# Coupled harmonics and the one-hot's counting row read from PSUM by VectorE; the weighted sweeps' one-hot compare made per tile

## The reference, cut to what matters

```
edge_index = stack([src, dst])
x = layernorm(x + L0(x, edge_index, edge_attr_4, edge_attr_32, ...))     # weighted: per-edge MLP gives 4 x 8 x 8 weights
x = layernorm(x + L1(x, edge_index, edge_weight1, edge_attr_3, edge_attr_5, W))   # coupled
x = layernorm(x + L2(x, edge_index, W1, b1, W2, b2))                     # two convolutions
x = layernorm(x + L3(x, edge_index, edge_attr_4, edge_attr_8, ...))      # weighted, MLP of three layers

# coupled layer: harmonics sh (1 + 3 + 5 values per edge) times the source's features, mixed by W
for idx, (le, ln, lo) in enumerate(COMBOS):
    base = einsum('ijk,ei,emj->emk', CG[le, ln, lo], sh[le], feats[ln])
    msg[lo] = msg[lo] + einsum('io,eik->eok', W[idx], base)
agg0 = segment_sum(msg[0], dst);  agg1 = segment_sum(msg[1], dst)
```

## Time and profile before

| | |
|---|---|
| median of 3 runs | 26496.01 us (26398.16 to 26498.13) |
| profiled execution, first to last instruction (span) | 21541.2 us |
| profiled execution, time outside its span | not recorded |
| PE / weight loads | 13199.4 us busy (61%) / 9916.4 (46%) |
| DVE | 9294.4 us (43%) |
| ACT | 2665.2 us (12%) |
| POOL | 15690.7 us (73%) |
| mean granted TensorE clock | 0.678 of 2.4 GHz |

### The profile page before, as it was taken

The page is one execution under the profiler, slowest core; times in us unless marked ns, Lnnn a source line. Parts: engine busy times, 40 slices in busy tenths (PEclk is TensorE's granted clock), DMA queues, the critical chain, the costliest instruction groups (busy, mean ns, idle before and its releaser), DMA issues. The chain is left out here.

```text
span 21541.2 us, 268058 instructions
## 1 busy us (share of the span) xinstructions
PE 13199.4 (61%) x71680; PEld 9916.4 (46%) x71680; DVE 9294.4 (43%) x22443; ACT 2665.2 (12%) x6512; POOL 15690.7 (73%) x15707
## 2 busy tenths in 40 slices
PE   8999999976666666512222223212221399999999
PEld 5666666666666666511111112111111266666666
DVE  7777777833333333211111111111111388888885
ACT  2333333310000000100000000000000022222222
POOL 6777777747777777677777774777777677777774
PEclk8988988955555555555555555555555599999997
DMA  1111111111111111100000010000000111111111
GB/s 32 26 26 26 26 26 26 27 13 16 16 16 16 16 16 16 15 14 14 14 14 14 14 13 12 14 14 14 14 14 14 15 17 18 18 17 18 17 17 13
DMA packets 1290570, 372.67 MB, mean 17 GB/s; under 512 B 1002127, under 2 KB 1269819, under 8 KB 1290172
## 3 DMA queue, kind: packets, MB, share of 16 engines
q0 software_dynamic: 502400, 258.23, 7.7%
q1 hardware_dynamic: 788150, 114.20, 3.3%
HBM read 363.02 MB, written 8.00 MB: 17 GB/s over the span
## 5 line engine op out<-in xcount | busy, mean ns | idle before, releaser
L323 POOL DMA_INDIRECT conv_rows<-conv_rows,conv_idx x6280 | 5927.4, 944 | 2245.2 <-issue 1912.6
L753 PE MATMUL conv_win<-conv_onehot,conv_rows 128*32 128x64 f32 x12560 | 1572.6, 312 | 6305.3 <-DMA conv_rows<-conv_rows,conv_idx 6254.9
L753 PEld LDWEIGHTS conv_win<-conv_onehot,conv_rows 128*32 128x32 f32 x12560 | 1298.6, 169 | 6579.0 <-issue 4974.1
L323 POOL DMA_INDIRECT coupled_rows<-x_after_weighted,coupled_idx x3140 | 3302.0, 1052 | 1206.1 <-issue 955.0
L323 POOL DMA_INDIRECT weighted_rows<-in_x,weighted_idx x3140 | 3251.5, 1036 | 1105.3 <-issue 937.4
L323 POOL DMA_INDIRECT weighted_rows<-x_after_convolved,weighted_idx x3140 | 3209.0, 1022 | 1064.2 <-issue 953.7
L458 PE MATMUL weighted_weights_ps<-weighted_w_out,weighted_hidden 128*128 128x256 f32 x12580 | 3781.5, 426 | 21.1 <-DVEq L550 21.1
L669 PE MATMUL coupled_win<-coupled_onehot,coupled_prod 128*125 128x64 f32 x12560 | 2762.0, 418 | 1531.0 <-DVE coupled_prod L705 1531.0
L669 PEld LDWEIGHTS coupled_win<-coupled_onehot,coupled_prod 128*125 128x125 f32 x12560 | 2677.4, 330 | 1615.6 <-issue 834.5
L458 PEld LDWEIGHTS weighted_weights_ps<-weighted_w_out,weighted_hidden 128*128 128x128 f32 x12580 | 2256.0, 199 | 1818.0 <-issue 1617.9
L767 DVE TENSOR_TENSOR acc<-acc,conv_win 32x64 f32 x1256 | 262.3, 209 | 6237.3 <-PE conv_win L753 6237.3
(11 more groups left out here) (133 smaller groups left out, 8636.9 us busy)
## 6 DMA issues: line engine op xcount, KB each, us to landing
conv_rows<-conv_rows,conv_idx POOLq DMA_INDIRECT x6280, 2.3
weighted_feat<-in_ef SPq DMA_DIRECT2D x632, 80.0 KB
weighted_rows<-in_x,weighted_idx POOLq DMA_INDIRECT x3140
coupled_rows<-x_after_weighted,coupled_idx POOLq DMA_INDIRECT x3140, 2.3
weighted_rows<-x_after_convolved,weighted_idx POOLq DMA_INDIRECT x3140, 2.3
weighted_idx<-in_src_blocks SPq DMA_DIRECT2D x1264, 2.5 KB
weighted_sh<-in_sh SPq DMA_DIRECT2D x1264, 10.0 KB
conv_idx<-in_src_blocks SPq DMA_DIRECT2D x1264, 2.5 KB, 1.6
```

The costliest lines, as they stand in the source:

```text
L323: pool.indirect_dma_start(rows[s][:, t, :], None, table, bass.IndirectOffsetOnAxis(ap=idx[s][:, t:t + 1].bitcast(U32), axis=0))\
L753: mm = pe.matmul(win_ps[s % 2][0:FEAT, 0:WINDOW], rows[s][:, t, :], onehot[s][:, t, :], start=(t == 0), stop=(t == TILES - 1))
```

## The change

Three edits:

1. In the coupled sweep the harmonics are staged to PSUM. A new ACT program waits for a slot's load, and then copies the slot's `sh` (128 x 45) to one of two PSUM tensors `sh_ps`; the copy for block n + 2 is made when the message of block n is ready. DVE's two products read `sh_ps` in place of `sh` and wait for `sh_ready` in place of `loaded`.
2. In the coupled sweep and the convolutions the counting row is a PSUM tensor. The compare keeps its form.
3. In the weighted sweeps the counting row stays in SBUF. The compare of a block is five `tensor_scalar` operations of 64 columns, one per tile, in which the local target is a per-partition scalar operand, in place of one `tensor_tensor` of 320.

```diff
--- before.py
+++ after.py
@@ -332,7 +332,7 @@
 
         self.dve, self.k, self.iota, self.base_f, self.base, self.stepped = dve, k, iota, base_f, base, stepped
         dve.memset(k["acc"][0:parts[0], 0:parts[1], :], 0.0).then_inc(stepped, 1)
-        dve.tensor_copy(iota[:, :], k["iota0"][:, :]).then_inc(stepped, 1)
+        dve.tensor_copy(iota, k["iota0"][:, :]).then_inc(stepped, 1)
         dve.memset(base_f[:, :], float(NODES)).then_inc(stepped, 1)
         dve.wait_ge(stepped, 3)
         dve.tensor_copy(base_f[:, 1:BLOCKS + 1], k["lo"][:, :]).then_inc(stepped, 1)
@@ -343,7 +343,7 @@
     def next_window(self, p):
 
         dve = self.dve
-        dve.tensor_scalar(self.iota[:, :], self.iota[:, :], float(WINDOW), None, ALU.add).then_inc(self.stepped, 1)
+        dve.tensor_scalar(self.iota, self.iota, float(WINDOW), None, ALU.add).then_inc(self.stepped, 1)
         dve.tensor_scalar(self.base_f[:, :], self.base_f[:, :], float(WINDOW), float(NODES), ALU.add, ALU.min)\
            .then_inc(self.stepped, 1)
         dve.wait_ge(self.stepped, p * 3 + 7)
@@ -353,6 +353,14 @@
     def bases(self, block, count=SLOTS):
 
         return nc_values(self.k["nc"], self.base[0:1, bass.ds(block + 1, count)])
+
+    def one_hot_tiles(self, dst, block):
+
+        for t in range(TILES):
+            last = self.dve.tensor_scalar(
+                dst[:, t, :], self.iota,
+                self.k["local"][:, bass.ds(block, 1), t:t + 1].rearrange("p b t -> p (b t)"), None, ALU.is_equal)
+        return last
 
     def one_hot(self, dst, block):
 
@@ -545,7 +553,7 @@
                 dve.wait_ge(params, PARAMS)
                 dots = w_out[0:HID + 1, 0:2 * MUL * MUL].rearrange("h (o q i) -> h o q i", q=2, i=MUL)[:, :, 0, :]
                 dve.tensor_scalar(dots, dots, float(1 / np.sqrt(3.0)), None, ALU.mult).then_inc(ones, 1)
-                win = Windows(dve, k, iota, base_f, base, stepped, (P, 2))
+                win = Windows(dve, k, iota[:, :], base_f, base, stepped, (P, 2))
                 dve.sem_inc(summed, 1)
                 dve.sem_inc(w_used, 2)
 
@@ -569,7 +577,7 @@
                             x, h, scaled = rows[s], sh[s], scaled_pair[s % 2]
                             harm = h[:, :, 1:4][:, :, None, :].broadcast_to([P, TILES, MUL, 3])
                             vecs = x[:, :, MUL:].rearrange("p t (i m) -> p t i m", m=3)
-                            win.one_hot(onehot[s], i * SLOTS + s).then_inc(vec, 1)
+                            win.one_hot_tiles(onehot[s], i * SLOTS + s).then_inc(vec, 1)
                             dve.wait_ge(gathered[s], g * (16 * TILES) + 16 * TILES)
                             dve.wait_ge(loaded[s], g * 48 + 48)
 
@@ -633,8 +641,12 @@
         idx, sh = ring("idx", [P, TILES], I32), ring("sh", [P, TILES, HARM])
         rows, onehot = ring("rows", [P, TILES, FEAT]), ring("onehot", [P, TILES, WINDOW])
         prod = ring("prod", [P, TILES, 2 * OCH])
-        iota, base_f, base = sb("iota", [P, WINDOW]), sb("base_f", [1, BLOCKS + SLOTS]), sb("base", [1, BLOCKS + SLOTS], I32)
+        base_f, base = sb("base_f", [1, BLOCKS + SLOTS]), sb("base", [1, BLOCKS + SLOTS], I32)
         win_ps = [ctx.enter_context(nc.psum_tensor(f"coupled_win{b}", [P, 512], F32)) for b in range(2)]
+        iota = ctx.enter_context(nc.psum_tensor("coupled_iota", [P, 512], F32))[:, 0:WINDOW]
+        sh_ps = [ctx.enter_context(nc.psum_tensor(f"coupled_sh_ps{b}", [P, 512], F32))[:, 0:TILES * HARM]
+                 .rearrange("p (t c) -> p t c", c=HARM) for b in range(2)]
+        sh_ready = sem("sh_ready")
         loaded, gathered = [sem(f"loaded{s}") for s in range(SLOTS)], [sem(f"gathered{s}") for s in range(SLOTS)]
         msg_ready, spread, summed, stepped, ones = sem("msg_ready"), sem("spread"), sem("summed"), sem("stepped"), sem("ones")
         started, ended = sem("started"), sem("ended")
@@ -671,6 +683,21 @@
                                                start=(t == 0), stop=(t == TILES - 1))
                         mm.then_inc(spread, 1)
 
+            @block.scalar
+            def _(act):
+                def stage(s, turn):
+
+                    act.wait_ge(loaded[s], turn * 32 + 32)
+                    nc.scalar.activation(sh_ps[s % 2], sh[s][:, :, :], ACT.Copy).then_inc(sh_ready, 1)
+
+                turns = Turns(act, k)
+                stage(0, 0)
+                stage(1, 0)
+                with turns.flat() as g:
+                    for s in range(SLOTS):
+                        act.wait_ge(msg_ready, g * SLOTS + (s + 1))
+                        stage((s + 2) % SLOTS, g + (s + 2) // SLOTS)
+
             @block.vector
             def _(dve):
                 for s in range(SLOTS):
@@ -694,10 +721,10 @@
                         bases = win.bases(i * SLOTS)
                         for s in range(SLOTS):
                             n = g * SLOTS + s
-                            x, h = rows[s], sh[s]
+                            x, h = rows[s], sh_ps[s % 2]
                             win.one_hot(onehot[s], i * SLOTS + s)
                             dve.wait_ge(gathered[s], g * (16 * TILES) + 16 * TILES)
-                            dve.wait_ge(loaded[s], g * 32 + 32)
+                            dve.wait_ge(sh_ready, n + 1)
                             dve.tensor_tensor(
                                 prod[s][:, :, 0:4 * FEAT].rearrange("p t (c f) -> p t c f", c=4),
                                 h[:, :, 0:4][:, :, :, None].broadcast_to([P, TILES, 4, FEAT]),
@@ -721,8 +748,9 @@
         ring = lambda n, shape, dt=F32: [sb(f"{n}{s}", shape, dt) for s in range(SLOTS)]
         idx = ring("idx", [P, TILES], I32)
         rows, onehot = ring("rows", [P, TILES, FEAT]), ring("onehot", [P, TILES, WINDOW])
-        iota, base_f, base = sb("iota", [P, WINDOW]), sb("base_f", [1, BLOCKS + SLOTS]), sb("base", [1, BLOCKS + SLOTS], I32)
+        base_f, base = sb("base_f", [1, BLOCKS + SLOTS]), sb("base", [1, BLOCKS + SLOTS], I32)
         win_ps = [ctx.enter_context(nc.psum_tensor(f"{name}_win{b}", [P, 512], F32)) for b in range(2)]
+        iota = ctx.enter_context(nc.psum_tensor(f"{name}_iota", [P, 512], F32))[:, 0:WINDOW]
         loaded, gathered = [sem(f"loaded{s}") for s in range(SLOTS)], [sem(f"gathered{s}") for s in range(SLOTS)]
         msg_ready, spread, summed, stepped = sem("msg_ready"), sem("spread"), sem("summed"), sem("stepped")
         started, ended = sem("started"), sem("ended")
```

## The result

The changed kernel took 27256.72 us (median of 4 runs, 27225.93 to 27286.64), the kernel before 26479.83 beside it: ratio 1.0296, 95% interval 1.0275 to 1.0318. It is 3% slower; 26,140 and a gain had been forecast.

The account below looks back on a forecast made before the run. POOL, issuing gathers back to back, was taken to pace the coupled sweep. Harmonics -335 and compare -15 gave -350 us, carried from the profiled execution to the 26,496 median: 26,140, range 25,950 to 26,490.

Parts of the forecast that it names:

- Step 1: Coupled sweep: products reading harmonics from PSUM no longer hold gathers, 1052 to 944 ns each; -335 us.
- Step 2: Coupled sweep: ACT's copy per block and DVE's wait on it cost 0, as ACT is idle and copies ahead.
- Step 3: Coupled sweep: POOL still sets the pace at 25.0 us a turn, PE's chain at most 22.4, 2.6 us over.
- Step 4: Coupled sweep and convolutions: the compare's counting row in PSUM changes nothing; 0 us.
- Step 5: Weighted sweeps: five small compares take 0.6 us against 0.48, the 0.12 covered; gather effect taken as -15 us.
- Rival C: Weighted sweeps: small compares hold no gather, -145 us more, 26,016; sign: weighted0 gathers under 1000 ns; chance 0.15.
- rival A: Weighted sweeps: small compares block gathers wherever they meet, 754 us less the 335, 26,915, slower; chance 0.10.
- Step 6: Last weighted stage: PE works without pause at 6.60 us a block, so a freed POOL only waits; 0 us.
- The 4955 us between span and median: Whole kernel: unexplained excess of the runs' median 26496 over the profiled span 21541; the 350 us carried over unchanged.
- a factor: Whole kernel: case that everything was 1.23 times as slow in the timed runs; gain -431 us, 26,065.
- PE's clock in the weighted stages: Weighted stages: case that the 4955 us come from PE at its lower clock; the coupled sweep's 335 would stand.
- Rival D: Coupled sweep: meets PE's chain before POOL's floor, half the gain left, 26,310; chance 0.06.

Follow-up runs that it names:

- e3: Kernel before with only the coupled harmonics staged by ACT into PSUM, chip without late releases: ratio 0.9832, 21220 us against 21572.
- e7: Kernel before, unchanged, profiled again on a chip without late releases: 21580 us.
- e6: The whole changed kernel, unchanged, on another chip, without late releases: 21108 us, ratio 0.9799 to the kernel before.
- e16: Kernel before with ACT's PSUM copies of coupled harmonics made and waited for, DVE still reading SBUF; chip without late releases: ratio 0.9968.
- e17: Same kernel as e16 (copies made and waited for, DVE still reading SBUF), on a chip with late releases: ratio 1.0063.
- e4: Kernel before with only the counting row in PSUM, in the coupled sweep and both convolutions; no late releases: ratio 0.9980.
- e2: Kernel before with only the compare per tile in the two weighted sweeps, chip without late releases: ratio 0.9919.
- e18: Kernel before with only the compare per tile, as e2 once more, again on a chip without late releases: ratio 0.9941.
- e12: Kernel before with nine more ACT activations in every second weighted block, so PE idles; chip with late releases: 28,753 us.
- e14: Kernel before with only the compare per tile, plus the same ACT delay as e12; chip with late releases: 28,848 us.
- e9: Changed kernel with PE made late by repeated matmuls, no late releases otherwise: 27,037.91 us, ratio 1.0025 to the kernel before with the same late PE.
- e15: Kernel before with only the coupled harmonics in PSUM, as e3, on a chip with late releases: 27,567.68 us, ratio 1.0171.

## Why the prediction was wrong

Wrong in its result, and nearly right for the execution that it was read from.

- **Step 1 (harmonics), -335 us.** Without late releases: -353 in e3, coupled stage -330 from e7 to e6, gathers at 944. Right in mechanism and size. **Step 2 (ACT's copies), 0**: 0.997 in e16, with 0.21 us for a copy in e6; right there, but 1.0063 in e17.
- **Step 3 (POOL sets the pace, with 2.6 us a turn over).** Right without late releases: 24.9 us a turn in e6, POOL waiting for "issue". With them it fails: 33 to 37 us a turn, set by PE's late releases.
- **Step 4 (counting row), 0.** e4: 0.998; convolutions 3918 as before.
- **Step 5 (compare), -15.** Mis-sized: -193 us in e2 and -105 in e18. Rival C was right that the small compares hold no gather, and its -145 lies between the two, though weighted0's mean gather stayed at 1001 to 1008 ns, not under 1000 as its sign had it. By the Trainium skill, "SBUF — State Buffer", section Who interferes with whom, a tensor_scalar in a two-port mode would lock GpSimd out (rival A); the 553 gathers at 944 ns do not show it. Whether this compare runs in such a mode no run here shows: its next operation starts 0.163 us later, where that of L346, as wide, starts after 0.10. DVE's own price I had too low: the five start 0.163 us apart and take 0.95 us together (median in e6), not 0.6, and 0.95 - 0.48 = 0.47 us a block were covered, not 0.12.
- **Step 6 (weighted3 at PE's 6.60), 0.** 6.66 us a block (e7) to 6.60 (e6).

Their sum, -350, stands against -418 measured on a chip without late releases. That nearness is in part luck, since the compare was mis-sized and the parts measured alone (605 us) do not add up to the whole. **The step that failed is this one of the sum:** "I carry the 350 us over as they are", because in the coupled sweep "that stage is paced by POOL with PE at the lower level already". The 4955 us between span and median were not a factor, nor PE's clock in the weighted stages: by the late profiles 920 to 980 us of such a difference lie in the coupled sweep (e12, e14), 2 x 700 in the convolutions (where PE is busy 16% of the time), the rest in the weighted sweeps. They go with PE's late releases, and behind a late PE POOL's shorter gathers are worth nothing (e9, late by hand) or less than nothing (e15). Rival D named PE's chain, but priced it as half the gain left; rival A had the sign, by a mechanism that isn't there. The range rested on the assumption that the unexplained part keeps its pace-setter.

What is shown: the harmonics alone lose 1.7% under late releases, in the coupled sweep, whose turns then all take 36.5 to 36.7 us. What is only argued: that the turn locks to the pauses because POOL, being early, starts each turn in the same place. No run tests that order of things. What is open: what makes PE's releases late, why the lock falls on the longest turn, and the rest of the first measurement's 777 us beyond e15's 457, where the kernel before was itself 600 us quicker than on the other chips with late releases; its coupled sweep there was not profiled.

## What to carry to other kernels

If the timed runs are far from the profiled execution (here 23%), a sum made in the profile is worth nothing for them until it is known which stage holds the difference and which engine sets the pace there: forecast the two cases apart, each with its own sign. Making an engine quicker that then waits for a late event can cost time, not just fail to gain it (e15: 1.7%). And a gain of 2% that was measured on one chip should be measured on a second.

## What the runs showed of the hardware

- In four of nine measurements (the first and those of e12 to e14, e15 and e17) PE's releases came late: up to 20.0 us after the last matmul's start in the coupled sweep (e12) and 22.4 us in the convolutions (e17), at an unchanged granted clock of 0.50, in the convolutions with PE busy only 16% of the time. Now and then the matmuls themselves started some 2.1 us apart instead of 0.21. On those three later chips the kernel before takes 5.5 ms more than the 21.5 ms elsewhere.
- A gather that has started is not held, and does not slow DVE: in the convolutions of the kernel before, whose compare L359 has two SBUF inputs, 1251 of 1256 compares start while a gather runs. They take 0.49 us as the others do, and the gathers the 0.943 of the floor.
- In weighted3 of the profile after PE is busy 3263 of 4000 us and the granted clock is 0.86; without late releases (e6) it is busy all 3500 us of a window at 1.00. Its gaps are such as this one, in which ACT waits for PE's late release:

```profile
24008.94 0.72 PE L454 MATMUL weighted_hid_ps<-weighted_first,weighted_w_mid 128*64 128x320 f32 x2 [0.75 <-issue]
24013.97 0.52 ACT L516 ACTIVATE weighted_hidden<-weighted_hid_ps,weighted_b_mid 64x320 f32<-64x320 f32 x1 [5.18 <-remote]
```

- A 64-wide compare with a column as its scalar starts every 0.163 us and takes 0.25 us in the median (0.28 in the mean), where the immediate form took 0.19.
